# Two-layer adapter FFN on one core: gathers between the result stores, and the layer-0 softmax moved within ACT's and DVE's order

## The reference

```python
def cond(x, A, B, ids):                       # per sequence, rank 16
    return einsum('bnr,bor->bno', einsum('bni,bri->bnr', x, B[ids]), A[ids])

def ffn(c, W, b, A, Bm, router):              # 4 experts of rank 8
    gates = softmax(c @ router.T + router_bias)      # layer 0 also adds log(prior)
    return c @ W.T + b + sum_e 2 * gates_e * (c @ A_e.T) @ Bm_e

x = x + ffn0(cond(x, L0_A, L0_B, id0))        # 8 adapters to pick from
x = x + ffn1(cond(x, L1_A, L1_B, id1))        # 64 adapters to pick from
```

## Time and profile before

| what | value |
|---|---|
| median of 3 runs | 334.89 us (334.2 to 335.64) |
| profiled execution | 334.41 us |
| its span, first to last instruction | 332.7 us |
| PE, DVE, ACT, POOL busy | 307.0, 220.1, 186.4, 63.3 us |
| HBM read, written | 39.15 MB, 16.78 MB |

### The profile page before, as it was taken

The page is one execution under the profiler, slowest core; times in us unless marked ns, Lnnn a source line. Parts: engine busy times, 40 slices in busy tenths (PEclk is TensorE's granted clock), DMA queues, the critical chain, the costliest instruction groups (busy, mean ns, idle before and its releaser), DMA issues.

```text
span 332.7 us, 6476 instructions
## 1 busy us (share of the span) xinstructions
PE 307.0 (92%) x2048; PEld 284.4 (85%) x2048; DVE 220.1 (66%) x476; ACT 186.4 (56%) x384; POOL 63.3 (19%) x58
## 2 busy tenths in 40 slices
PE   5994998799989998999979999999999999999894
PEld 4453998589978998999979999999999999899783
DVE  2156887686738766686658666777668676864556
ACT  1446976946546565755466465646575657461520
POOL 5600000620042103320143003320332024200000
PEclk9999899999999999999999999999999999999999
DMA  7999973006870388126840587037811783041006
GB/s 267 345 365 381 347 208 156 0 8 167 300 224 0 104 243 302 51 60 212 286 139 0 158 284 250 2 103 244 299 47 55 255 292 92 0 193 62 1 0 252
DMA packets 30773, 56.16 MB, mean 169 GB/s; under 512 B 3633, under 2 KB 20050, under 8 KB 30754
## 3 DMA queue, kind: packets, MB, share of 16 engines
q1 hardware_dynamic: 29666, 52.97, 48.3%
q0 software_dynamic: 1088, 2.97, 2.5%
HBM read 39.15 MB, written 16.78 MB: 168 GB/s over the span
## 4 chain that ended last, share of the span: by engine, by line
issue 41%; PE 20%; DMA 13%; POOL 12%; DVE 6%; ACT 3%; SPq 2%; POOLq 1%; DVEq 0%; ACTq 0%
POOL xs_lo L952 8%; DMA out<-xraw 6%; DMA xraw<-x_in 6%; PE ps_d L307 3%; PE ps_d L309 3%; PE ps_d L308 3%; POOL a1s_lo L952 2%; DVE xs_lo L740 2%; DVE xraw L942 2%; PE ps_d L545 1%; PE ps_p L307 1%; PE ps_d L547 1%; ACT res L574 1%; SPq L253 1%; SPq L251 1%
## 5 line engine op out<-in xcount | busy, mean ns | idle before, releaser
L952 POOL TENSOR_TENSOR xs_lo<-xraw,xs_hi 128x512 fp32r<-128x512 f32 x28 | 36.0, 1290 | 182.5 <-ACT xs_hi L574 182.4
L307 PE MATMUL ps_d<-w1s_hi,a1s_hi 128*128 128x384 f32 (+1 forms) x192 | 63.9, 333 | 0.0
L309 PE MATMUL ps_d<-w1s_hi,a1s_lo 128*128 128x384 f32 (+1 forms) x192 | 62.0, 323 | 0.0
L308 PE MATMUL ps_d<-w1s_lo,a1s_hi 128*128 128x384 f32 (+1 forms) x192 | 61.9, 322 | 0.0
L942 DVE SCALAR_TENSOR_TENSOR xraw<-ps_d,lp,xraw 128x512 f32<-128x512 f32 x60 | 43.6, 748 | 22.5 <-PE ps_d L547 22.5
L574 ACT ACTIVATE xs_hi<-xraw 128x512 fp32r<-128x512 f32 x60 | 36.0, 626 | 26.4 <-DMA xraw<-x_in 25.9
L307 PE MATMUL ps_p<-xs_hi,bst_hi 128*128 128x256 f32 x120 | 36.5, 304 | 6.2 <-DVE bst_lo L740 2.4
L308 PEld LDWEIGHTS ps_d<-w1s_lo,a1s_hi 128*128 128x128 f32 x192 | 36.2, 189 | 0.0
L307 PEld LDWEIGHTS ps_d<-w1s_hi,a1s_hi 128*128 128x128 f32 x192 | 36.1, 188 | 0.0
L309 PEld LDWEIGHTS ps_d<-w1s_hi,a1s_lo 128*128 128x128 f32 x192 | 36.1, 188 | 0.0
L308 PE MATMUL ps_p<-xs_lo,bst_hi 128*128 128x256 f32 x120 | 34.5, 288 | 0.0
(11 more groups left out here) (227 smaller groups left out, 702.9 us busy)
## 6 DMA issues: line engine op xcount, KB each, us to landing
out<-xraw SPq DMA_DIRECT2D x31, 512.0 KB, 3.5
xraw<-x_in SPq DMA_DIRECT2D x28, 512.0 KB, 5.0
w_plain<-w SPq DMA_DIRECT2D x16, 512.0 KB, 8.9
abraw<-ab_tab SPq DMA_DIRECT2D x64, 128.0 KB, 2.1
b0raw<-b_tab SPq DMA_DIRECT2D x64, 64.0 KB, 2.0
xraw<-x_in POOLq DMA_DIRECT2D x4, 512.0 KB, 11.0
a_plain<-a SPq DMA_DIRECT2D x1, 512.0 KB, 3.6
out<-xraw SPq DMA_DIRECT2D x2, 256.0 KB, 2.7
```

What stands on the lines that cost most here:

```text
L307: pe.matmul(acc, lh, rh, start=first, stop=False, skip_group_check=True)
L308: pe.matmul(acc, lh, rl, start=False, stop=False, skip_group_check=True)
L309: return pe.matmul(acc, ll, rh, start=False, stop=final, skip_group_check=True)
L952: return pool.tensor_tensor(dst, whole, high.bitcast(F32), ALU.subtract)
```

## The change

Three edits. SP issues the 16 gathers in four groups (6, 4, 4 and 2 DMAs), one ahead of each store, and an x load follows its store at one store's more distance: load 0 stands behind store 2 instead of store 1, and loads 2 and 3 behind the loop. ACT does the exponent of layer 0 right behind the `ht` and `he` copies, then `wide_high(1)`, and x chunks 0 and 1 behind that; in step 0 `wide_high(0)` also moves behind the exponent. DVE does `softmax(0)` ahead of `wide_low(0)`, with the low parts of `ht` and `he` inside it, between the subtraction of line 881 and the wait for the exponent.

```diff
                     picks = pick(g + 2)
                     sp.wait_ge(a_lo, g + 2)
-                    gather(picks, range(GROUP))
                 for i in range(CH - 1 if last else CH):
+                    if ahead:
+                        gather(picks, (range(0, 3), range(3, 5), range(5, 7), range(7, 8))[i])
                     sp.wait_ge(d_out, KT * g + KC * (i + 1))
...
-                    if ahead and i > 0:
-                        sp.wait_ge(stored[i - 1], 16 * g + 16)
-                        load_x(g + 2, par, i - 1)
+                    if ahead and i > 1:
+                        sp.wait_ge(stored[i - 2], 16 * g + 16)
+                        load_x(g + 2, par, i - 2)
                 if ahead:
-                    sp.wait_ge(stored[CH - 1], 16 * g + 16)
-                    load_x(g + 2, par, CH - 1)
+                    for i in (CH - 2, CH - 1):
+                        sp.wait_ge(stored[i], 16 * g + 16)
+                        load_x(g + 2, par, i)
...
-                wide_high(0)
-                act.wait_ge(ht_done, g + 1)
+                if first:
+                    act.wait_ge(ht_done, g + 1)
+                else:
+                    wide_high(0)
+                    act.wait_ge(ht_done, g + 1)
                 copy(ht[:, 0, :], ps_t[:, 0:P]).then_inc(ht_hi, 1)
                 copy(he[0:LR, :], ps_t[0:LR, P:2 * P]).then_inc(ht_hi, 1)
+                softmax_exp(0)
+                if first:
+                    wide_high(0)
+                wide_high(1)
                 if not last and not first:
                     split_x(g + 1, 1 - par, 0, [0, 1])
-                softmax_exp(0)
-                wide_high(1)
                 act.wait_ge(htx_done, g + 1)
...
                                       ALU.subtract).then_inc(sm_step, 1)
+                    if layer == 0:
+                        dve.wait_ge(ht_hi, 2 * g + 2)
+                        low(ht[:, 1, :], ps_t[:, 0:P], ht[:, 0, :])
+                        low(he[ELO, :], ps_t[0:LR, P:2 * P], he[0:LR, :]).then_inc(ht_lo, 1)
                     if layer == 1 and not last:
...
+                softmax(0)
                 wide_low(0)
-                dve.wait_ge(ht_hi, 2 * g + 2)
-                low(ht[:, 1, :], ps_t[:, 0:P], ht[:, 0, :])
-                low(he[ELO, :], ps_t[0:LR, P:2 * P], he[0:LR, :]).then_inc(ht_lo, 1)
-                softmax(0)
                 wide_low(1)
```

## The result

| kernel | median us (range, runs) | ratio to before, 95% interval |
|---|---|---|
| before | 335.11 (332.82 to 337.97, 20) | 1 |
| changed | 340.18 (335.92 to 343.19, 20) | 1.0112 [1.008, 1.0143] |

The ratio, and every median from the experiments on, leaves out executions over 1.5% above the fastest of their kernel: over the other 14 the changed kernel's median is 338.94 us, and of e10's runs one of 427.73 us, at a mean granted clock of 0.655, is left out.

A forecast was written before the change was run, and what follows sets the result against it. PE was taken as the bound, busy 307 of 332.7 us, so only its idle time could yield gain. Part 1's 6.0 plus the `cf` credit's 0.6, other parts 0, made 6.6 us: 328.3 us, range 326.9 to 331.4.

The forecast's parts named there:

- Part 3: SP's new order: two x loads leave 2.3 and 1.1 us earlier, last gather 2.4 us later; costed at 0.
- I take 4.4 us: SP's last gather, behind a load and a store: assumed time from issue to landing, all gathers in at 233.5.
- G + 6.1: DVE's last softmax product `l_done`, predicted 6.1 us after all gathers are in, through high copy, low halves and softmax.
- threshold of 234.2: Latest time in step 5 for all gathers to be in without PE waiting; landing within 5.1 us of issue.
- sign of being wrong: ACT's line 588 copy released by a DMA over 5 us after the last gather, PE idle at the turn.
- `ht_lo` never late: PE at line 478: `ht_lo` comes before `l_done`, so it was claimed not late either; no cost.
- ring rule: DMA engines consume rings in order; by it alone the last gather could not be counted before load 0.
- gathers the bound: Rival at ACT's `split_b`: gather takes 6.9 us, PE stalls 1.8 us in six steps, 339.1 us; chance 0.06.
- Part 1: Exponent ahead of x copies: PE's weight-load wait for `l_done` at line 445 (the turn) goes; 6.0 us gain.
- Part 2: ACT's x copies 0 and 1 behind `wide_high(1)`: PE's projection not delayed, 1.2 us in time; cost 0.
- `cf` credit: DVE's 4.8 us of waits for ACT's copies into `cf`: 0.6 us gained, bounds 0 and 1.8.
- Part 4: Step 0: what PE gains at the turn it loses waiting for POOL's x halves; 0, bounds -1.0 and +0.3.

The follow-up runs named there:

- e10: Changed kernel with x load 0 behind the last gather and `split_b` behind the exponent (ACT) and `softmax(0)` (DVE) in steps 1 to 6; 328.57 us, ratio 0.980.
- e3: Changed kernel with all gathers issued ahead of store 2 and x load 0 in SP's queue; 328.75 us, ratio 0.977.
- e5: Changed kernel with store 2 moved behind the last gather, x load 0 still ahead of it; 331.93 us, ratio 0.989.
- e2: Kernel before with only the new ACT and DVE orders, SP's order old; 334.17 us, ratio 0.994.
- e4: Changed kernel with x load 0 moved one place, behind the last gather, store 2 still ahead of it; 327.88 us, ratio 0.974.
- e11: e4 with ACT's x copies 0 and 1 back ahead of the exponent; 333.29 us, ratio 0.994.
- e1: Kernel before with only the new SP order, ACT and DVE orders old; 364.29 us, ratio 1.081.
- e6: Changed kernel with `split_b` behind the exponent on ACT and behind `softmax(0)` on DVE in steps 1 to 6; 329.71 us, ratio 0.980.
- e7: Changed kernel run again unaltered for a second profile; 338.92 us, ratio 1.010.
- the first profile: Profiled execution of the unaltered changed kernel, the fastest of its 20; 335.92 us.
- e8: Changed kernel run again unaltered for a third profile; 340.34 us.

## Why the prediction was wrong

**The step that failed is Part 3, the term "I take 4.4 us" for the last gather's landing.** It came out at 6.0 us in step 5, and at 5.6 to 6.0 in the six steps. Beside it a smaller term was off: I had the gather leave at 229.1, with 0.53 us for each of the 15 before it. It left at 229.99, because in each group of gathers behind a store or load one takes 0.60 to 0.67 us on SP instead of 0.33. So G, when all gathers are in, was 236.0 instead of 233.5. The next term held: `l_done` came at G + 5.6 where I had G + 6.1. The threshold of 234.2 for a free landing was thus some 0.5 us too strict, and G passed it by over a microsecond even so. The turn waits in all of steps 1 to 6. The prediction's own sign of being wrong was this one: ACT's copy released by a DMA over 5 us behind the last gather, with PE idle at the turn. The prediction also had `ht_lo` never late; in the changed kernel PE waits 5.3 us for it at line 481, since the low parts of `ht` and `he` hang on the same late copy.

How the 4.4 came about is the lesson of it. The nearest row for a DMA behind a load and a store was x load 1, 6.9 us. I took it for the upper bound and scaled it down, since the gather is 192 KB (its pair; the last DMA alone is 128) and the load 512. But the time is not the gather's own: e3 shows the same DMA at 2.7 us, e5 at 5.4 with the load ahead. What is paid is the rest of the load, which landed 6.7 us from its issue, 0.7 before the gather; the gather's size takes nothing off that. The bound was 0.9 too high and the estimate 1.6 too low: the size argument led away from the answer. Part 3 also read step 5 alone, where PE released ACT's copy. In steps 1 to 3 of the kernel before the gathers released it already, 2.2 to 2.6 us from the last issue.

**The ring rule was in the text and had no chance of its own.** The prediction said that by that rule the gather couldn't be counted before load 0, and that the sum would turn if the load took over 6 us. A rule by which the sum turns should have been weighed by the rows at hand (load 1: 6.9 us), and that weighing would have given "gathers the bound" far more than 0.06.

**The rival had place and price.** "ACT's `split_b` at a step's start, G = 236.0, 339.1 us", decided from a landing of 6.2 us. Measured: the same wait, G = 236.0, 340.18 us over all executions, 338.94 over the 14. That G agrees to the tenth is luck: the issue came 0.9 us later and the landing took 0.9 less. The working of 1.8 us a step in six steps is 10.8; the profiles show 9.6 to 10.7 of turn waits.

**Part 1 was right.** The turn wait of 6.0 us in steps 1 to 5 goes when the exponent no longer stands behind x: 0.4 us of the 7.0 is left in e2 and e4, in step 0. e4, the change with one load moved by one place in SP's queue, has a median of 327.88 us, against the 328.3 forecast for the change. That nearness is in part luck: on its chip the kernel before took 336.62, so e4 gained 8.7 us where 6.6 was forecast.

**Part 2 was right on cost and small on gain.** In e4 PE waits for POOL's low halves at the projection for 1.7 us in two waits, both in step 0, so copies 0 and 1 are in time behind `wide_high(1)`. The `cf` credit of 0.6 us (bounds 0 and 1.8) was too small for what the small waits gave back. From the turn of step 1 to that of step 7 before takes 310.69 - 95.95 = 214.74 us, of which steps 2 to 5 hold 6.0 - 1.77 = 4.2 of turn wait, so 210.5 are left. e4 takes 302.77 - 93.98 = 208.8. So 1.7 us went beside the turn wait; how they divide over `cf`, POOL and DVE's stretched scaling no run separated. I had also given the move of the copies no value of its own beside the softmax's; e11 puts it at 5 to 7 us.

**Part 4 was right.** In step 0, PE takes 6.30 us from line 481 to the first projection (52.52 to 58.82), against 6.45 before (53.53 to 59.98). The turn comes sooner behind its product, and the wait for POOL is 1.51 instead of 1.03: gained at one, given back at the other.

**What no term held is the clock, and it does not explain the miss.** Losses differ by run and by kernel: medians of 4.3 to 4.7 us for before on three chips, 4.2 for changed, 5.6 for e4, 18.1 for e1. In e4 that hid a little of the gain: by medians its span less the loss is 320.9 us, against 330.6 for before on its chip, 9.7 less, of which the clock took 0.9 back. Why e4 loses more to the clock than before, outside any turn wait, is open. The miss itself is in the waits. From the first turn to the last, less one stretch at 0.50, the changed kernel's profile has 257.4 us, and the forecast was 255.9 - 6.6 = 249.3: 8.1 too few. Turn waits of 9.2 (9.6 less the 0.4 of step 0) less the 1.1 by which the `cf` credit was too small (1.7 - 0.6) are 8.1. The other two profiles have 259.3 and 259.1, some 1.8 more, of which 0.6 to 1.1 are turn waits and the rest was not placed.

## What to carry to other kernels

When a DMA moves to a place behind a large load in the same queue, cost its landing as that load's (in these traces 0.5 to 0.7 us behind it), whatever its own size, and compare with the nearest measured landing behind such a load without shading it down. Then ask which in-order engine reads it first, and what stands behind that reader: either the load goes behind the small transfer (e4) or the reader goes behind the critical chain (e6), and one of the two is enough to free that chain. A change in two halves may pay only whole: here each half alone gave 0.6% or 0.7% at best, one of them cost 8% in its first form, and the two together gave 2.6%.

## What was not expected of the hardware

- The same 128 KB gather lands 2.6 to 4.4 us from its issue with no x load of 512 KB ahead of it (e3, e4) and 5.4 to 6.0 with one (e5, changed), then always 0.5 to 0.7 us behind that load.
- At the end of step 4 SP needs 0.58 to 0.76 us for one gather of each group behind a store (the second, in the changed kernel and e3 to e5), where the others take 0.33. Behind the load it was the first in the changed kernel (0.67) and none in e5. The cause is open.
- A granted clock of 0.50 for 3.4 us (or 6.8) behind turn waits: in e1 behind the turn waits of all six steps, in e7 behind its longest (1.91 + 0.51) alone, in the first profile and e8, whose longest at line 481 are 1.6 and 1.4, behind none. Such a stretch also stands where no turn wait is, at 65.5 in the changed kernel and at 33.0 before.
- DVE's scaling of 128x16 elements takes 0.17 us alone and 0.81 to 0.82 beside POOL's subtraction.
